# A gathering graph pass in three bf16 parts: a kept fp32 table row becomes 768 bytes, a summing step one bf16 matmul

## The reference, cut to what matters

```python
loop_message = h @ loop_weight
xw = jnp.einsum('ni,rio->rno', h, W)
msg = xw[rel, src] + bias_term[rel]
gate = jax.nn.sigmoid(jnp.sum(msg * gw[rel], axis=-1) + gate_bias[rel, 0])
agg = jax.ops.segment_sum(msg * gate[:, None], dst, num_segments=n_nodes)
node_repr = agg + loop_message
return jax.nn.relu(node_repr)
```

## Time and profile before

| | |
|---|---|
| median of 3 runs | 2308.58 us (2307.8 to 2309.11) |
| profiled execution, span | 2719.1 us |
| busy, TensorE matmul / weight load | 1467.8 / 1028.2 us |
| busy, VectorE / ScalarE | 939.2 / 630.7 us |
| busy, GpSimd | 1356.5 us |
| mean granted TensorE clock | 0.762 of full speed |

### The profile page before, as it was taken

How to read it: one execution, slowest core, us unless ns; L and a number is a source line. 1 busy time by engine, 2 the same in 40 slices (tenths; PEclk the granted TensorE clock), 3 DMA queues, 4 the chain that set the end, 5 groups by cost and what they waited for, 6 DMA issues and landing times.

```text
span 2719.1 us, 32229 instructions
## 1 busy us (share of the span) xinstructions
PE 1467.8 (54%) x7630; PEld 1028.2 (38%) x7755; DVE 939.2 (35%) x2174; ACT 630.7 (23%) x1678; POOL 1356.5 (50%) x1567
## 2 busy tenths in 40 slices
PE   5666999999626666655774243333334323232233
PEld 3444454454425555444553132322323223232232
DVE  9877221226513333323343332332333212121122
ACT  3777000000112232222331233333334000000000
POOL 4000167500256555554533666666665566666664
PEclk9999999999768787777787666767667655665566
DMA  1000011002312222222222122222222211111111
GB/s 26 0 0 5 16 11 10 6 1 49 86 42 77 76 90 76 83 75 67 73 85 74 45 67 63 65 66 68 60 66 67 52 48 46 50 47 47 49 48 39
DMA packets 126215, 137.46 MB, mean 51 GB/s; under 512 B 80273, under 2 KB 97433, under 8 KB 123000
## 3 DMA queue, kind: packets, MB, share of 16 engines
q0 software_dynamic: 40896, 81.94, 12.0%
q1 hardware_dynamic: 85240, 54.54, 6.6%
HBM read 91.88 MB, written 44.52 MB: 50 GB/s over the span
## 4 chain that ended last, share of the span: by engine, by line
PE 36%; another core or an unknown queue 26%; issue 23%; DVE 9%; ACT 4%; DVEq 1%; POOL 1%; ACTq 0%; DMA 0%; POOLq 0%; SPq 0%
PE acc L1320 15%; PE acc L1591 6%; PE acc L1518 6%; PE acc L1488 5%; DVE feat L2037 1%; ACT adj L1789 1%; DVE adj L2025 1%; PE acc L1210 1%; PE acc L1212 1%; ACT adj L1713 1%; ACT acc L1717 1%; PE misc L1256 1%; POOL adj L1002 1%; DVE adj L2374 1%
## 5 line engine op out<-in xcount | busy, mean ns | idle before, releaser
L1002 POOL DMA_INDIRECT adj<-table,adj x832 | 792.0, 952 | 476.8 <-issue 241.0
L1002 POOL DMA_INDIRECT adj<-tablex,adj x416 | 392.8, 944 | 366.1 <-ACT adj L1766 166.7
L1591 PE MATMUL acc<-adj 128*128 x1760 | 329.2, 352 | 453.1 <-issue 247.8
L1591 PEld LDWEIGHTS acc<-adj 128*128 128x128 f32 x1760 | 298.9, 259 | 438.0 <-issue 437.5
L1320 PE MATMUL acc<-adj,feat 128*128 (+2 forms) x2031 | 401.3, 353 | 13.2 <-issue 9.4
L1518 PE MATMUL acc<-adj 128*128 128x128 f32 x1664 | 259.6, 320 | 79.8 <-issue 58.7
L1518 PEld LDWEIGHTS acc<-adj 128*128 128x128 f32 x1664 | 247.4, 232 | 116.0 <-issue 115.7
L2025 DVE TENSOR_TENSOR adj<-acc,drel 128x768 f32<-128x768 f32 (+1 forms) x148 | 138.4, 945 | 414.9 <-remote 285.4
L1320 PEld LDWEIGHTS acc<-adj,feat 128*128 (+1 forms) x2100 | 185.9, 98 | 217.5 <-issue 13.4
L1789 ACT ACTIVATE adj<-adj 128x128 f32<-128x128 f32 x832 | 261.9, 388 | 22.4 <-DVEq L2628 18.6
L1464 PE MATMUL acc<-ident,adj 128*128 128x128 f32 x48 | 21.6, 450 | 435.4 <-issue 327.4
(11 more groups left out here) (351 smaller groups left out, 1425.3 us busy)
## 6 DMA issues: line engine op xcount, KB each, us to landing
table<-adj SPq DMA_DIRECT2D x24, 1024.0 KB
adj<-table,adj POOLq DMA_INDIRECT x834, 2.2
table<-adj SPq DMA_DIRECT2D x25, 512.0 KB
adj<-tablex,adj POOLq DMA_INDIRECT x416
table<-adj SPq DMA_DIRECT2D x25, 64.0 KB
out_dram<-adj SPq DMA_DIRECT2D x24, 64.0 KB
temp<-in_x_dram SPq DMA_DIRECT2D x4, 256.0 KB, 3.3
wrel<-node_rep SPq DMA_DIRECT2D x16, 64.0 KB
```

The costliest lines, as they stand in the source:

```text
L1002: pool.indirect_dma_start(ring[:, p_, 0:D], None, rows_, bass.IndirectOffsetOnAxis(ap=gidx[:, p_:p_ + 1], axis=0)).then_inc(msgs_in[third_ ...
L1591: last = nc.tensor.matmul(acc[:, bass.ds(blk[s], width)], hot[:, c, j, :], ring_flat[:, bass.ds(place[s], width)], start=False, stop=True, ...
```

## The change: table rows of pass 3 as three bf16 parts

- The table of pass 3 becomes bf16 with 384 columns: three parts that add up to the fp32 value, 768 bytes a row in place of 512.
- `table_parts` in pass 2 writes additions and gate products into a buffer `scaled`, then makes the parts: copy to bf16, subtract, copy to bf16, subtract, each for two halves of 128x512, eight more operations a block. SP writes 768 KB per block in place of 512.
- The gathers of pass 3 fetch 768 bytes a row, to other places in SBUF (`ring3`, over the old ring, the free space before it and a part of the one-hot buffers). Their number and indices stay.
- The one-hot matrices of pass 3 are bf16 (`hot3`). A step is one bf16 matmul of 384 columns. The places of the steps are computed once, in turn 1 of pass 2 (`places_of_parts`, eight operations on one partition); the second `next_places` goes.
- `block_sum` in pass 3 adds the three sums with two more dependent additions of 128x128.
- A second form of the passes, taken on other inputs only, is adapted as well.

```diff
-        table3 = dram("table3", (NA * R3, D))
+        table3 = dram("table3", (NA * R3, PARTS3 * D), BF16)
...
-                sp.dma_start(rows3[bass.ds(b.num(P), rows_of(b)), :], stage[0:rows_of(b), b.r, 0:R3 * D]).then_inc(stage_out[b.r], 16)
+                sp.dma_start(rows3[bass.ds(b.num(P), rows_of(b)), :], parts_stage[0:rows_of(b), b.r, 0:R3 * W3]).then_inc(stage_out[b.r], 16)
...
-                        pool.indirect_dma_start(ring[:, p_, 0:D], None, rows_,
+                        pool.indirect_dma_start(ring3(p_) if ph == 3 else ring[:, p_, 0:D], None, rows_,
...
-                        last = nc.tensor.matmul(acc[:, bass.ds(blk[s], width)], hot[:, c, j, :], ring_flat[:, bass.ds(place[s], width)],
+                        one, rows_ = (hot, ring_flat) if ph == 2 else (hot3, bigb)
+                        last = nc.tensor.matmul(acc[:, bass.ds(blk[s], width)], one[:, c, j, :], rows_[:, bass.ds(place[s], width)],
...
+                elif ph == 3 and not general:
+                    whole = acc[:, b.r * KB:b.r * KB + W3].rearrange("p (s f) -> p s f", s=PARTS3)
+                    nc.vector.tensor_tensor(y1[:, :], whole[:, 0, :], flat(rest), ALU.add).then_inc(parts_made, 1)
+                    hold(dve, parts_made, b.num(2, SPLITS * BLOCKS + 1))
+                    nc.vector.tensor_tensor(y1[:, :], y1[:, :], whole[:, 1, :], ALU.add).then_inc(parts_made, 1)
+                    hold(dve, parts_made, b.num(2, SPLITS * BLOCKS + 2))
+                    nc.vector.tensor_tensor(y1[:, :], y1[:, :], whole[:, 2, :], ALU.add).then_inc(sum_read, 1)
...
-                    dve.wait_ge(stage_out[b.r], slots_used(2, b))
+                    after(dve, rows_set, b.num())
                     for j in range(2):
                         dve.wait_ge(prod_full[j], blocks_seen(2, b, 1))
-                        nc.vector.tensor_tensor(stage[:, b.r, j * KB:(j + 1) * KB], psum_bank(4 + j),
+                        nc.vector.tensor_tensor(scaled[:, j * KB:(j + 1) * KB], psum_bank(4 + j),
...
+                        nc.vector.tensor_tensor(half(j), half(j), gate[:, j * R3 // 2:(j + 1) * R3 // 2].unsqueeze(2).to_broadcast([P, R3 // 2, D]),
+                                                ALU.mult).then_inc(parts_made, 1)
+                    dve.wait_ge(stage_out[b.r], slots_used(2, b))
+                    for n in range(2):
+                        for j in range(2):
+                            hold(dve, parts_made, b.num(SPLITS, 4 * n + j + 1))
+                            nc.vector.tensor_copy(part(j, n), half(j)).then_inc(parts_made, 1)
+                        for j in range(2):
+                            hold(dve, parts_made, b.num(SPLITS, 4 * n + j + 3))
+                            nc.vector.tensor_tensor(part(j, 2) if n else half(j), half(j), part(j, n), ALU.subtract
+                                                    ).then_inc(rows_set if n == j == 1 else parts_made, 1)
...
+                        if ph == 2 and isinstance(t.k, int) and t.num() == 1:
+                            places_of_parts()
...
                 one_pass(2, general)
-                next_places(general)
                 one_pass(3, general)
```

More of the change, by code:

```diff
@@ L54 @@
 TPT = sum(SIZES)
+W3, SPLITS = 3 * 128, 9
 AHEAD_T = 3
@@ L353, in gnn @@
         assert o0 + R1 * TW // 2 + 4 + R3 * D <= NP + PARTS3 * NP // 2
+        scaled = feat[:, NP:NP + R3 * D]
+        place_w, place_over, place_sum = (feat[0:1, NP + R3 * D + i * WSTEPS:NP + R3 * D + (i + 1) * WSTEPS] for i in range(3))
+        places3 = feat[0:1, NP + R3 * D + 3 * WSTEPS:NP + R3 * D + 4 * WSTEPS].bitcast(I32).rearrange("p (i s) -> p i s", i=TURNS)
+        assert R3 * D + 4 * WSTEPS <= TW + 2 + TW // 2 + TW // 2 + 2 + R1 * TW // 2
+        wide_rows = feat[:, NP:NP + SPT * (W3 // 2)].bitcast(BF16).rearrange("p (s w) -> p s w", s=SPT)
         o1 = FNB * FG * FCOLS
@@ L978, in body @@
                         hold(pool, ggidx_set, ordinal + 1)
+                        in_parts = table is table3
                         for j in range(n):
-                            pool.indirect_dma_start(ring[:, c * G + j, 0:D], None, table,
+                            pool.indirect_dma_start(wide_rows[:, c * G + j, :] if in_parts else ring[:, c * G + j, 0:D], None, table,
                                                     bass.IndirectOffsetOnAxis(ap=gidx2[:, c, j:j + 1], axis=0)
@@ L984, in body @@
                         hold(pool, gmsgs_in[c], z * (16 * of_c) + t.num(16 * G, 16 * n))
-                        if weight is None:
+                        if in_parts:
+                            for j in range(n):
+                                first = nc.gpsimd.tensor_tensor(ring[:, c * G + j, 0:D], wide_rows[:, c * G + j, 0:D],
+                                                                wide_rows[:, c * G + j, D:2 * D], ALU.add)
+                            first.then_inc(parts_made, 1)
+                            hold(pool, parts_made, t.num(NB, SPLITS * BLOCKS + c + 1))
+                            for j in range(n):
+                                last = nc.gpsimd.tensor_tensor(ring[:, c * G + j, 0:D], ring[:, c * G + j, 0:D],
+                                                               wide_rows[:, c * G + j, 2 * D:3 * D], ALU.add)
+                            last.then_inc(gweighted, 1)
+                        elif weight is None:
                             pool.sem_inc(gweighted, 1)
@@ L1169, in _, with load_row @@
             nc.tensor.transpose(acc[0:1, 5 * KB + 256:5 * KB + 256 + P], peak[:, 0:1], ident[:, :]).then_inc(ends_ps, 1)
-            def load_row(t, lo, n, top):
+            def load_row(t, lo, n, top, table=walk_i):
                 _, vals = nc.values_load_multi_w_load_instructions(
-                    walk_i[0:1, bass.ds(t.num(), 1), lo:lo + n].rearrange("p i w -> p (i w)"), engines=[mybir.EngineType.PE],
+                    table[0:1, bass.ds(t.num(), 1), lo:lo + n].rearrange("p i w -> p (i w)"), engines=[mybir.EngineType.PE],
                     min_val=0, max_val=top,
@@ L1570, in sums @@
                     upto = blk[WAITS:]
-                place = load_row(t, PLACES, sum(sizes), (RING - 1) * RW)
+                if ph == 2:
+                    place = load_row(t, PLACES, sum(sizes), (RING - 1) * RW)
+                else:
+                    place = load_row(t, 0, sum(sizes), third1 + TPT * W3, places3)
                 def landed(u, k):
@@ L1674, in passes @@
                 pe.wait_ge(sum_read, 2 * BLOCKS)
-                pe.wait_ge(tab_set, 2)
+                if not general:
+                    pe.wait_ge(tab_set, 9)
                 one_pass(3, general)
@@ L2470, in table_parts, with half, part @@
             def table_parts(ph, b):
+                def half(j):
+                    return scaled[:, j * KB:(j + 1) * KB].rearrange("p (r w) -> p r w", w=D)
+                def part(j, s):
+                    return parts_stage[:, b.r, j * KB * PARTS3:(j + 1) * KB * PARTS3].rearrange("p (r s w) -> p r s w", r=R3 // 2, s=PARTS3)[:, :, s, :]
                 own = rest[:, bass.ds(b.num(), 1), :].rearrange("p b f -> p (b f)")
@@ L2609, in next_places, with places_of_parts, step @@
                 nc.vector.engine_nop().then_inc(tab_set, 1)
+            def places_of_parts():
+                def step(ins):
+                    step.n += 1
+                    ins.then_inc(tab_set, 1)
+                    hold(dve, tab_set, step.n)
+                step.n = 1
+                whole = float(1 << 23)
+                w, over, total = (p_.rearrange("p (i s) -> p i s", i=TURNS) for p_ in (place_w, place_over, place_sum))
+                froms = (third1, third2 - TPT * W3, third0 - 2 * TPT * W3, third0c - (2 * TPT + PARTS_AT[3]) * W3)
+                jumps = [(float(slot * W3), float(froms[n + 1] - froms[n])) for n, slot in enumerate((TPT, 2 * TPT, 2 * TPT + PARTS_AT[3]))]
+                step(nc.vector.tensor_scalar(w, walk_i[0:1, :, PLACES:PLACES + SPT], 1.0 / RW, whole, ALU.mult, ALU.add))
+                step(nc.vector.tensor_scalar(w, w, whole, float(W3), ALU.subtract, ALU.mult))
+                step(nc.vector.tensor_scalar(over, w, jumps[0][0], jumps[0][1], ALU.is_ge, ALU.mult))
+                step(nc.vector.scalar_tensor_tensor(total, over, float(froms[0]), w, ALU.add, ALU.add))
+                step(nc.vector.tensor_scalar(over, w, jumps[1][0], jumps[1][1], ALU.is_ge, ALU.mult))
+                step(nc.vector.tensor_tensor(total, total, over, ALU.add))
+                step(nc.vector.tensor_scalar(over, w, jumps[2][0], jumps[2][1], ALU.is_ge, ALU.mult))
+                step(nc.vector.tensor_tensor(places3[:, :, :], total, over, ALU.add))
             def pair_weights():
```

33 lines of the change are left out of this document (21 added, 12 removed).

## The result

The changed kernel took 2321.02 us (median of 4 runs, 2320.33 to 2322.76), the kernel before 2308.19 (4 runs, 2306.41 to 2309.11): ratio 1.0059, 95% interval 1.0045 to 1.0074. It is slower, by 12.8 us, a little under half of the 27.4 forecast. The order of the causes was wrong too: the prediction had 15 us for VectorE holding up GpSimd and 12 for the end of the second pass, and the second is the larger.

The account below looks back on a forecast made before the run. GpSimd's gathers, one start every 1.248 us, were taken to bound all three passes. Tail 0.5, larger gathers 0, VectorE holding up GpSimd 15 and the second pass's end 12 sum to 27.5; 2308.6 + 27.5 = 2336 us, range 2309 to 2372.

Parts of the forecast that it names:

- VectorE holds up GpSimd: Second pass: the new subtractions lengthen gathers, 0.7 us a block over 22 blocks, +15 us (0 to 25).
- The end of the second pass: GpSimd's wait for the whole table grows by three blocks' splits and a larger last write, +12 us (5 to 16).
- The bound: All three passes go at GpSimd's pace, one gather start per beat of 1.248 us, which sums to 2303.3 us.
- rival 1: Slower consumers were the bound after all, so lighter third-pass steps make it faster, about 2300 us; chance 0.09.
- Rival 5: VectorE's order becomes the loop of the second pass, 2360 us and more; chance 0.04.
- Gathers of 768 bytes: GpSimd's third-pass gathers fetch half again the bytes at the same count, at a cost of 0.
- rival 3: A row of 768 bytes takes two descriptors, so third-pass gathers grow by 41 us, 2377 us; chance 0.07.
- the four subtractions are two such pairs, so 0.4 us at least: Second pass: each pair of SBUF-input VectorE operations delays gathers about 0.2 us, a floor per block.
- Rival 2: No change: the subtractions' fixed phase to the beat meets no gather, table early enough, 2309 to 2313 us; chance 0.12.
- Rival 4: Second pass: copies hold GpSimd for their whole length, 39 us, 2369 us in all; chance 0.08.
- The cover's slack: End of the second pass: 20 gathers, 25.0 us, cover 22 us of work before the table is ready, some 3 to spare.
- The tail: After the last gather: 8 lighter steps gain 0.9 to 1.4 us, dependent adds cost 1.6, +0.5 us (-0.5 to +1.5).

Follow-up runs that it names:

- the first profile: The profiled execution of the kernel before that the prediction was read from, unchanged code; span 2719.1 us.
- experiment 9: The changed kernel with every TensorE step of the third pass issued twice: 2321.48 us, ratio to the kernel before 1.0067.
- experiment 2: The changed kernel with the eight splitting operations of every block on 2 columns each, so without the split: 2309.91 us.
- experiment 4: The changed kernel with the split in full for blocks 0 to 21 alone, 2 columns for the last three: 2313.05 us.
- experiment 6: The changed kernel with only the subtractions of blocks 0 to 21 in full, all other splitting operations on 2 columns: 2328.96 us.
- experiment 7: The changed kernel with two 512-column copies joined into one of 1024, and two subtractions likewise, in blocks 0 to 21: 2346.55 us.
- experiment 5: The changed kernel with only the copies of blocks 0 to 21 in full, all other splitting operations on 2 columns: 2317.36 us.
- experiment 8: The kernel before with TensorE adding the table part's bias, so that VectorE's one multiplication per half reads PSUM: 2302.94 us.
- experiment 10: The changed kernel with TensorE adding the table part's bias and VectorE's multiplication reading PSUM: 2319.35 us, ratio to the kernel before 1.0054.

## Why the prediction was half right

**The bound: right.** The sum at 1.248 us a beat gave 2303.3; the span of before without stalls is 2306.3, and from the second pass on GpSimd waits 0.9 us in it beside its own issue. The stalls of the first profile were its own, rival 1 has no ground, and experiment 9 shows that TensorE, whose steps the change makes lighter, is covered. Rival 5 falls too: after the change GpSimd waits 2.1 us for indices from the second pass on.

**Gathers of 768 bytes: right** (946 against 944 ns, about 0.8 us in all where I had 0), so rival 3 falls.

**"VectorE holds up GpSimd", +15 us: the step that failed.** The mechanism was right and its size was not: 3.8 us between the two traces, 3.1 by experiments 2 and 4, about 0.15 a block where I took 0.7. What failed is "the four subtractions are two such pairs, so 0.4 us at least": over the 22 blocks the subtractions took 0.45 us from gathers together, 0.02 a block, and the copies 3.2. The long gathers stood beside copies, not beside the new subtractions as forecast. A pair has no fixed price: what a gather loses is what is left of the operation in progress shortly after its start, if that began first. I had worked that out as a mean over random meetings, and used the traced pairs as a floor; but the meetings are not random. In the traced blocks VectorE's multiplications are released by ScalarE's gate, and that stands behind the weighting of tiles that a gather has just delivered:

```profile
1647.30 1.28 ACT L1826 ACTIVATE adj<-adj 128x128 f32<-128x128 f32 x4 [3.48 <-DMA adj<-table,adj]
1648.60 1.28 ACT L1853 ACT_TABLE_LOAD   x1
1649.89 0.21 ACT L1853 ACTIVATE adj<-adj 128x8 f32<-128x8 f32 x1
```

So the gathers set the phase of the work that holds them, and a pair of subtractions (two starts 0.60 apart, 1.2 us in all) is about as long as the beat of 1.25: once one gather starts at the seam of two operations, the next ones do too. The records of the changed kernel agree: of the 22 gathers that met the multiplications of blocks 0 to 21, 19 began between 0.06 us before and 0.10 after the start of the second one; then 22 gathers began 0.13 us into the second copy of a pair, and 22 began 0.53 to 0.54 us into the first subtraction of a pair, which is 0.68 long. Rival 2 had named this ("their phase to the beat is fixed"), and for this term it was the better story. Experiments 6 and 7 show that nothing protects it: 0.36 a gather with the copies gone, 25.5 us more with the operations joined. The small price is luck of the phase; in either of those kernels 15 us would have been too little (17 us more gather time than before in experiment 6, 30 in experiment 7).

**Copies against subtractions.** In the Trainium skill the page "SBUF — State Buffer", section "Who interferes with whom", calls the port pair that VectorE and GpSimd share an exclusive lock, and infers that a two-input operation takes only its read side and leaves the generation of descriptors alone. The lock agrees with the runs where VectorE comes first: the gather waits to the end of the operation (experiments 5 to 7). Where the gather comes first it does not: VectorE loses 0.05 us there, not the gather's length. The inference does not agree either: subtractions held gathers as copies did. The section also says that a two-input operation contends with a GpSimd instruction that reads SBUF. A gather reads its indices there (`gidx`), so this may be the case at hand, but no run here tells a gather's reads from its writes. Rival 4, which priced copies at their whole length, falls too, since a gather waits only for the rest of a copy.

**The end of the second pass, +12 us (5 to 16): right in kind, 9.65 in size.** The timeline of SP has the issues of the last two table writes, before and after:

```profile
1789.45 3.14 SPq L848 DMA_DIRECT2D table<-adj  x2
```

```profile
1799.77 6.75 SPq L869 DMA_DIRECT2D table<-adj  x2
```

Before, the last one ends 20.84 us behind the start of the pass's last gather (1771.75 to 1792.59), after 32.11 (1774.41 to 1806.52): 11.3 more, where I had 13.9. Timeline of VectorE and GpSimd at the end, after:

```profile
1782.05 0.76 DVE L2549 CAST adj<-feat 128x512 bf16<-128x512 f32 x2
...
1785.93 0.15 DVE L2479 COPY indeg<-acc 128x1 f32<-128x1 f32 x1
...
1810.36 0.94 POOL L1034 DMA_INDIRECT adj<-table,adj  x1 [9.35 <-DMA table<-adj]
```

A split takes 3.9 us (1782.05 to 1785.93), not 4.6: each operation starts about 0.08 us before the record of the one ahead ends, so two of 0.68 take 1.28. Three make 11.6. The cover's slack was nearly as forecast, 2.4 us where I had 3, but by two misses that cancel. After, the gather starts 3.84 us behind that issue (1806.52 to 1810.36); a write of before, if it took as long, would be there at 1796.4, which is 24.7 us behind the pass's last gather where I had 22. The gather behind the 20 began 27.0 us behind that gather where I had 25.0, since from one to the other there are 21 beats and VectorE held some of them:

```profile
1798.79 0.94 POOL L1002 DMA_INDIRECT adj<-table,adj  x1 [0.30 <-issue]
```

11.3 - 2.4 = 8.9, and the row shows 9.05 beyond the usual 0.30.

**The tail, +0.5 us (-0.5 to 1.5): 1.35.** The last 8 steps, before and after:

```profile
2295.77 3.77 PE L1591 MATMUL acc<-adj 128*128 x16 [2.97 <-DMA adj<-table,adj]
```

```profile
2308.09 2.74 PE L1627 MATMUL acc<-adj 128*128 x8 [3.75 <-DMA adj<-table,adj]
```

The 1.03 us gained lie in the range given, but the first sum starts only 0.59 us earlier behind the last gather (5.82 us before, 5.23 after); the two chains of sums and norms grew from 5.34 us (2297.97 to 2303.31) to 7.28 (2309.68 to 2316.96), 1.94 where I had 1.6.

By its own terms: 0.5 + 0 + 15 + 12 became 1.35 + 0 + 3.65 + 9.65 (the last holds the 0.8 or so of the larger rows), less 1.0 by which the first gather came earlier: 13.65 between the traces, 12.8 between the medians.

## What to carry to other kernels

Where two engines meet at a shared resource, bound the price from nothing to the longest operation and look at the phase before taking a middle: work that waits for the other engine's results meets it at the same point each time. Then the size, order and source of the operations can matter more than their total length: the same bytes of split cost 3 us in eight operations a block and 29 in four (3.1 and the 25.5 of experiment 7), and reading PSUM in place of SBUF took the wait away (experiment 8). And a cover of 27 us with 2.4 left passes on every further microsecond added in front of its end, however much the rest of the pass hides.

## What the runs showed of the hardware

- A gather of 944 ns waits only at one point, about 0.12 us after its start (0.944 less what follows the wait), for the end of a VectorE operation that began first and whose inputs are all in SBUF (copies of 512 and 1024 columns, multiplications, subtractions), and then takes 0.81 to 0.82 us more (0.91 beside the first subtraction of experiment 7). For the multiplications, to begin first meant 0.03 us ahead (experiments 5 and 6); but 13 operations of a normalization (L2510) that began up to 0.12 us ahead of a gather in the changed kernel held none, so the lead that it takes differs by operation. Where the gather comes first, VectorE's pair is longer by 0.05 (1.34 at 1650.23 for the usual 1.29), not by the gather's length. In the changed kernel 13 gathers began as a copy was just starting and lost nothing; there the copy's record is 0.44 to 0.46 long for the usual 0.41. The 23 gathers that met an addition reading PSUM (L2537) lost 0.01 us together. In experiment 10 nine gathers beside a multiplication reading PSUM did lose 0.6 us together; the records don't show why.
- With less work TensorE was granted a lower clock: 0.61 before, 0.52 after, 0.71 with the steps twice, over the windows of experiment 9, where 0.5 is the lower of its two levels (1.2 of 2.4 GHz). So a step fell only from 0.44 us (two records of 191.21/866) to 0.35 (156.01/448).
